# Image rows sent in the steps whose counts they need, and the rest of attention behind the last projection in an order of its own

## The reference

```
h = tok(x);  h = concat([h, txt], axis=1)                      # (32, 144, 192)
Q, K, V = einsum(W_Q|W_K|W_V, layernorm(h))                    # 12 heads of 64
h = h + W_O . (softmax(causal(Q K^T) / 8) V)
logits = layernorm(h) @ Wr;  topk_p, topk_i = top_k(softmax(logits), 2)
counts_before = cumsum(onehot, axis=0) - onehot                # over all rows, in order of the tokens
pos = counts_before at the row's expert;  keep = pos < 864     # capacity
h = h + sum over the 2 experts of  p * keep * (gelu(x @ w1[e] + b1[e]) @ w2[e] + b2[e])
```

## Time and profile before

| | |
|---|---|
| median of 3 runs | 860.81 us (859.82 to 864.62) |
| the profiled execution's own time | 862.2 us |
| its span | 860.5 us |
| attention steps with a projection, one step | 26.0 to 26.4 us |
| start of step 17 on PE | 533 us |
| last merge (pair 17) ends | 604.2 us |
| first load of the experts' block | 638.3 us |

### The profile page before, as it was taken

The page is one execution under the profiler, slowest core; times in us unless marked ns, Lnnn a source line. Parts: engine busy times, 40 slices in busy tenths (PEclk is TensorE's granted clock), DMA queues, the critical chain, the costliest instruction groups (busy, mean ns, idle before and its releaser), DMA issues. The chain is left out here.

```text
span 860.5 us, 25391 instructions
## 1 busy us (share of the span) xinstructions
PE 735.7 (85%) x9539; PEld 611.6 (71%) x9539; DVE 639.1 (74%) x1831; ACT 590.9 (69%) x1383; POOL 512.7 (60%) x612
## 2 busy tenths in 40 slices
PE   3689489999999999999999999975106899999994
PEld 3689257888788888888888888864103577777774
DVE  6892368899999999999999999876304666666651
ACT  1775168888888888888888888862105866766760
POOL 7666325556577687777877777775520154545555
PEclk9899699999999999999999999997557999999998
DMA  8961112111011221222212111220126466664223
GB/s 275 238 164 32 41 57 63 36 37 40 12 45 49 52 58 26 52 52 50 55 34 50 49 40 43 43 59 15 36 83 186 131 132 145 144 145 91 29 28 40
DMA packets 97034, 63.60 MB, mean 74 GB/s; under 512 B 48046, under 2 KB 91547, under 8 KB 96656
## 3 DMA queue, kind: packets, MB, share of 16 engines
q1 hardware_dynamic: 85648, 51.24, 23.0%
q0 software_dynamic: 11264, 10.74, 7.7%
HBM read 39.60 MB, written 24.15 MB: 74 GB/s over the span
## 5 line engine op out<-in xcount | busy, mean ns | idle before, releaser
L1892 POOL DMA_INDIRECT out<-y,tok x56 | 91.6, 1635 | 133.1 <-DVE y L1852 125.2
L1506 POOL TENSOR_TENSOR pl<-p,ph 128x384 f16<-128x384 f32 x144 | 131.6, 916 | 40.5 <-ACT ph L1361 38.0
L1343 ACT ACTIVATE p<-sps,nm 128x144 f32<-128x144 f32 (+1 forms) x432 | 128.7, 390 | 9.9 <-DVE nm L879 9.0
L658 PE MATMUL pj<-xt,wqkvh 128*128 128x256 f16 x648 | 108.4, 277 | 3.9 <-ACT xt L1397 1.5
L1866 DVE TENSOR_TENSOR h<-g,h 128x432 f16<-128x432 f32 x96 | 58.3, 607 | 68.8 <-ACT h L1810 68.7
L1555 POOL DMA_INDIRECT xg_d<-rows,sli x64 | 65.3, 1021 | 43.6 <-DVE sli L1206 34.4
L889 DVE COPY pt<-ptp 128x896 f16<-128x896 f16 (+1 forms) x144 | 86.2, 609 | 4.0 <-PE ptp L719 2.2
L917 DVE SCALAR_TENSOR_TENSOR qk<-pj,qk 128x512 f16<-128x512 f32 x108 | 73.8, 683 | 17.3 <-ACT qk L1326 16.4
L879 DVE TENSOR_REDUCE nm<-sps 128x3 f32<-128x432 f32 (+1 forms) x144 | 82.1, 591 | 4.5 <-PE sps L703 4.2
L1361 ACT ACTIVATE ph<-p 128x384 f16<-128x384 f32 x144 | 74.3, 537 | 15.0 <-PE ptp L719 13.6
L658 PE MATMUL pj<-xt,wqkvl 128*128 128x256 f16 x432 | 83.7, 276 | 0.0
(11 more groups left out here) (251 smaller groups left out, 2394.0 us busy)
## 6 DMA issues: line engine op xcount, KB each, us to landing
stage<-in_L_ffn_w SPq DMA_DIRECT2D x16, 384.0 KB
xg_d<-zrow SPq DMA_DIRECT2D x8, 588.0 KB, 6.1
xg<-xg_d SPq DMA_DIRECT2D x8, 588.0 KB
stage<-in_L_ffn_w SPq DMA_DIRECT2D x8, 576.0 KB, 6.0
out<-h SPq DMA_DIRECT2D x36, 96.0 KB
vi<-vimg_d SPq DMA_DIRECT2D x192, 16.2 KB
hin<-in_txt SPq DMA_DIRECT2D x16, 192.0 KB, 2.9
hres<-in_txt SPq DMA_DIRECT2D x16, 192.0 KB, 3.0
```

The lines of the kernel that those rows point to most:

```text
L658: mm = pe.matmul(bank[:, t * 256:(t + 1) * 256], (wqkvh, wqkvl)[w][:, b, c:c + P], xt[:, q, e, :], start=i == 0, stop=i == 4)
L1343: i = a.activation(p32[:, u % 2, r, lo:SEQ], sps[u % 2][:, r * SEQ + lo:(r + 1) * SEQ], ACT.Exp, bias=nm[:, u % 2, r:r + 1])
L1506: g.tensor_tensor(pl[:, u % 2, :, :], p32[:, u % 2, :, IT:SEQ], ph[:, u % 2, :, :], ALU.subtract).then_inc(S["pll"], 1)
L1892: g.indirect_dma_start(out, bass.IndirectOffsetOnAxis(ap=tok[0:n, 1 - par, u, :], axis=0), y2[0:n, 1 - par, u, :], None, compute_op=ALU.ad ...
```

## The change

Three things are changed. (1) `place_images` is cut into seven parts, `place_img(off, k)`, called for one tile at a time. Tile 0 is done in step 10, tile 1 in step 14 and sent (`send_img`) one step later; tile 2 in step 17; tile 3 at the end. (2) Step 17 (`TAIL`) is the last step of all engines but SP. It holds in one list what was in steps 17 to 22, in a new order. (3) Two waits of PE are finer: scores of units 0 and 1 wait for three items and not six, and pv waits for the one V item that it needs.

```diff
+TAIL = 17
@@ scores
+                if d < 2:
+                    wait(pe, "pjl", 10 * p + 3 * (d + 1))
                 if d == 0:
-                    wait(pe, "pjl", 10 * p + 6)
@@ pv
+                if u % 2 == 0:
+                    wait(pe, "pjl", 10 * p + 7 + u // 2)
                 if u == 0:
-                    wait(pe, "pjl", 10 * p + 10)
@@ step_pe: for s < TAIL as before, and
+            else:
+                scores(1, 0); transpose_a(2, 0, 0); transpose_p(2, 6); pv(2, 5); item(0, 0); transpose_p(2, 7); transpose_a(2, 0, 1); pv(2, 6)
...
+                scores(0, 0); item(0, 5); count(3); pv(1, 4); transpose_p(1, 6); transpose_a(1, 0, 0); item(0, 6); pv(1, 5)
...
+                transpose_p(0, 7); pv(0, 6); transpose_r(1); pv(0, 7); router(1); transpose_a(0, 1, 0); transpose_a(0, 1, 1); merge(0, 0)
+                merge(0, 1); count(1); transpose_r(0); router(0); count(0)
@@ step_dve
+            def place_img(off, k):
+                p = s - off
+                if not live(p) or image_after(p) is None:
+                    return
...
+                if k == 6:
+                    v.tensor_tensor(slia[:, t, :], sla[:, t, :], ova[:, t, :], ALU.add).then_inc(S["sldi"], 1)
...
-            if s == NPAIR:
-                place_images(v, ch, 0, 3)
...
+                logits(0); top(0); top_at(0); shift(0); chosen(0); one_hot(0); total(0); inv_total(0)
+                shares(0); counted(0); both(0); pick(0); inv_both(0); slot(0); fill(0); address(0)
+                place_img(0, 0); send_to(0); place_img(0, 1); next_ids(0); place_img(0, 2); place_img(0, 3); place_img(0, 4); place_img(0, 5)
+                place_img(0, 6)
+        def image_after(p):
+            t, r = divmod(p - NPAIR_A - 3, 4)
+            return t if r == 0 and t >= 0 else None
@@ step_pool
-            if s == NPAIR + 1:
-                wait(g, "sldi", 1)
-                for n in range(6):
-                    send_image(g, *divmod(n, 2))
...
+                send(2, 0, 0); low_a(0, 2); send(2, 0, 1); low_a(0, 3); send_img(4, 0); send(2, 1, 0); send(2, 1, 1); send_img(4, 1)
+                inv_h(0); send(1, 0, 0); send(1, 0, 1); low_r(0); send(1, 1, 0); send(1, 1, 1); send(0, 0, 0); send(0, 0, 1)
+                send(0, 1, 0); send(0, 1, 1); send_img(0, 0); send_img(0, 1)
@@ run
-            for s in range(-1, NPAIR + 5):
+            for s in range(-1, last + 1):
```

More of the change, by code:

```diff
@@ L827, in step_pe @@
                 wait(pe, "init", 1)
[L828 to L865, removed]
@@ L1208, in step_dve @@
             if s == 1:
                 wait(v, "init", 1)
[L1210 to L1272, removed]
@@ L1273, in step_dve @@
-            evac(1, 4)
-            evac(1, 5)
-            counted(3)
-            if s == NPAIR:
-                place_images(v, ch, 0, 3)
[L1279 to L1305, removed]
@@ L1452, in step_act @@
[L1452 to L1472, removed]
@@ L1473, in step_act @@
[L1473 to L1479, removed]
+            if s < TAIL:
+                high_r(3)
+                exps(1, 0)
+                high(0, 0)
+                evac_a(2, 0)
+                exps(1, 1)
+                high(0, 1)
+                cast(1, 0)
+                cast(1, 1)
+                cast_i(1, 0)
+                high(0, 2)
+                cast_i(1, 1)
+                high_a(2, 2)
+                evac_r(3)
+                exps(1, 2)
+                exps(1, 3)
+                high_a(2, 3)
+                high(0, 3)
+                cast(1, 2)
+                high(0, 4)
+                evac_a(2, 1)
+                cast_i(1, 2)
+                cast(1, 3)
+                cast_i(1, 3)
+                high(0, 5)
+                exps(1, 4)
+                exps(1, 5)
+                high(0, 6)
+                high_x(-1)
+                exp_r(3)
+                cast(1, 4)
+                cast_i(1, 4)
+                high(0, 7)
+                cast(1, 5)
+                cast_i(1, 5)
+                high_a(1, 0)
+                put_k(-1, 0)
+                put_k(-1, 1)
+                exps(1, 6)
+                high(0, 8)
+                exps(1, 7)
+                cast(1, 6)
+                high_a(1, 1)
+                cast_i(1, 6)
+                cast_i(1, 7)
+                cast(1, 7)
+                high(0, 9)
+                evac_x(-1)
+            else:
+                high_r(3); evac_a(2, 0); exps(1, 0); exps(1, 1); cast(1, 0); cast_i(1, 0); cast(1, 1); cast_i(1, 1)
+                high_a(2, 2); high(0, 0); exps(1, 2); exps(1, 3); cast_i(1, 2); evac_r(3); cast(1, 2); cast(1, 3)
+                cast_i(1, 3); high_a(2, 3); high(0, 1); exps(1, 4); exps(1, 5); evac_a(2, 1); cast(1, 4); high(0, 2)
+                cast_i(1, 4); cast(1, 5); cast_i(1, 5); high(0, 3); high_a(1, 0); exp_r(3); exps(1, 6); exps(1, 7)
+                high_a(1, 1); cast(1, 6); cast_i(1, 6); high(0, 4); cast(1, 7); cast_i(1, 7); exps(0, 0); exps(0, 1)
+                high(0, 5); evac_a(1, 0); high_r(2); cast(0, 0); cast(0, 1); cast_i(0, 0); cast_i(0, 1); high_a(1, 2)
+                high(0, 6); exps(0, 2); high(0, 7); evac_r(2); exps(0, 3); high_a(1, 3); cast(0, 2); cast_i(0, 2)
+                cast(0, 3); cast_i(0, 3); evac_a(1, 1); high(0, 8); exp_r(2); high(0, 9); high_a(0, 0); exps(0, 4)
+                exps(0, 5); cast(0, 4); cast_i(0, 4); exps(0, 6); cast(0, 5); cast_i(0, 5); cast(0, 6); cast_i(0, 6)
+                exps(0, 7); high_a(0, 1); cast(0, 7); cast_i(0, 7); evac_a(0, 0); high_r(1); high_a(0, 2); evac_r(1)
+                high_a(0, 3); exp_r(1); evac_a(0, 1); high_r(0); evac_r(0); exp_r(0)
@@ L1573, in step_pool, with send_img @@
[L1573 to L1585, removed]
-            if s == NPAIR + 1:
-                wait(g, "sldi", 1)
-                for n in range(6):
-                    send_image(g, *divmod(n, 2))
+            def send_img(off, kk):
+                p = s - off
+                if not live(p) or image_after(p) is None:
+                    return
+                t = image_after(p)
+                wait(g, "sldi", t + 1)
+                send_image(g, t, kk)
@@ L1666, in step_sp, with run @@
                 load_w1(sp, 0, 0)
[L1668 to L1670 removed]
+        def run(f, last=TAIL):
+            for s in range(-1, last + 1):
                 f(s, s % 2)
@@ L1683, in _ @@
                 run(lambda s, par: step_pool(g, s, par))
-                g.wait_ge(S["sldi"], 2)
-                for kk in range(2):
-                    send_image(g, 3, kk)
                 g.wait_ge(S["dsp"], 64 * (NPAIR - NPAIR_A))
```

250 lines of the change are left out of this document (212 added, 38 removed).

## The result

The changed kernel takes 856.36 us (median of 9 runs, 854.44 to 857.78), the kernel before 861.21 (9 runs, 859.82 to 864.62). The ratio is 0.9939 (0.9925 to 0.9954): 4.85 us less, where 14.2 was forecast and the range ended at 855. The profiled execution has a span of 854.2 us against 860.5.

What follows compares the result with a forecast made beforehand. TensorE was taken to bound the middle steps, with no engine full at the end. Gains of 9.5 and 5.7 less 1.0 took 14.2 us from the profiled 862.2, to 848.0, and 846.6 us as median; range 839.5 to 855.

Steps and rivals of the forecast that it cites:

- VectorE's work ahead of the last norm: From the start of step 17 to the last norm: 47.8 us of VectorE work.
- Part one: Tail from step 17 to the last merge: the new order ends the merge 9.5 us earlier (ends 15.4 and 0).
- The 90%: VectorE's busy share from step 17 to the last norm, giving 53.1 us for that stretch.
- The rest of part one: After the last norm: 4.4 us to the first merge, then 4.2 us for the merges.
- Part two: Image transfers at the end: two, not six, ahead of low_r of pair 17; 5.7 us gained (ends 6.4 and 4.5).
- Part three: Tiles 0 and 1 moved into middle steps: 1.0 us lost (0 to 4.4).
- The finer waits: Up to four semaphore waits in each of 16 middle steps: cost 0, bound 3.2 us.
- (b): Tail stays bound by one pair's chain, last norm no earlier: 856.1 us; chance 0.18, with what lies from 852 to 858.
- (c): Single address buffer makes VectorE wait for landed transfers in the last list: slower, up to 869.4 us; chance 0.04.
- signs for being right: Expected residual, low_r and step times, VectorE 85 to 93% busy, clock 1.00 until some 5 us before the merges.
- signs for being wrong: sli waiting over 1 us for a DMA, every middle step 0.2 us longer, or last norm 60 us after step 17's start.

Runs made afterwards that it cites:

- port_moved: The changed kernel with three small VectorE operations between SBUF tiles moved behind the rowmax they held up in the last list; 851.97 us.
- The two probes: The kernel before plus one unused VectorE operation in each of 14 middle steps: two SBUF inputs (867.30 us) or a one-input tensor_reduce (859.77 us).
- best2: best1 plus 36 unused matmuls in TensorE's gaps between the last pv and the two last merges; 848.58 us.
- best1: The kernel before with only the new order from step 17, all image work there, three VectorE operations moved later, token numbers made once at the start; 849.29 us.

## Why the prediction was wrong

The direction was right, the size was three times too large, and the range missed by 1.4 us. The step that failed most is VectorE's work ahead of the last norm, with the price of its waits for GpSimd; the cost in the middle failed with it. By its parts:

- **Part one, tail up to the merge: 9.5 us forecast, 3.4 measured.** The failing term is VectorE's work, 47.8 us. It was 55.2. The 90% that I took was not the error: it was 94%. The 7.4 us between are, but for the precision of my count, waits of small operations for GpSimd, shown as busy: to the last norm long operations exceed the shortest of their form by 10.7 us (11 operations), and 2.2 us of that kind were in the kernel before and so in my count. What I got wrong is their number and size. I took up to 0.6 us each, the remainder of one GpSimd operation, from xn, and 1.8 us in all. Nine of the eleven were of that size (0.3 to 0.75 us over the shortest); one_hot and next_ids were held through several operations, 2.3 and 3.2 us over it. In port_moved, where these two fell to 0.18 and 0.91 us, it is 53.4 us from the start of step 17 (536.4, as far behind the residual in step 16 as in the changed kernel) to the last norm (589.8), where I had forecast 53.1 and the changed kernel has 58.7. I had a rule for these waits: the Trainium skill (SBUF — State Buffer, Who interferes with whom) says that a VectorE instruction with two SBUF inputs contends with a GpSimd instruction that reads SBUF, that one in a two-port mode does too, and that tensor_reduce never does on this chip. The two probes agree with it (up to 2.85 us against 0.15). It speaks of a lock for a whole instruction; these traces show a wait through up to five.
- **The rest of part one held.** From the end of the last norm to the first merge 4.5 us (594.43 to 598.93; forecast 4.4), the merges 4.6 (forecast 4.2). The clock had fallen before them to 0.50 in 597 to 600, as taken. best2 shows 1.6 us for it (4.5 and 2.9 us), but whether transposes count as activity no run here tells apart.
- **Part two, transfers: 5.7 forecast, 6.3 measured**, with low_r where it was expected; no transfer was long.
- **Part three, the middle: 1.0 forecast, 4.3 measured**, the upper end of my range for it (4.4). I had taken VectorE's 1.6 us of idle time in a middle step as cover for 2.0 us of small operations. Step 10 got 2.2 us of busy time more (26.94 against 24.74), and the step is 1.8 us longer. But 1.6 of the 2.2 us are posa and one more address operation (sla, 0.59 and not 0.15 us) standing for GpSimd; that cost I had put at nothing here. Added operations as such were free in the probes' steps. And two transfers that I had called free cost 0.7 us, by what the traces show through xn, which is then held longer by GpSimd's chain. The finer waits cost nothing: middle steps without image work take 26.41 us in both.
- **Rivals.** (b), 856.1, gave the right time for another reason: the last norm did come earlier, by 3.2 us against the start of step 17. So the measured time, within 0.3 us of (b), says nothing for it. (c) did not happen; next_ids stood behind GpSimd's chain, not the address write behind a landing.
- **The signs.** Three of the signs for being right failed: the last residual came 67.9 us behind the start of step 17 and not 60 to 64, steps 10 and 14 were 1.8 and 1.3 us over their neighbours and not within 1, and VectorE was busy for 94% and not 85 to 93. low_r and the clock held. None of the signs for being wrong showed (the last norm came at 58.7 us, just under their 60), so they did not cover this failure.

## What to carry to other kernels

Do not read a duration as work before it is compared with the shortest of its form: here 11.6 us of VectorE's busy time in the tail, and most of what the address operations added to it in step 10, were waits for GpSimd. An operation's price on a nearly full engine depends on where it stands: 0.15 to 0.29 us more in a step with TensorE at 99% and VectorE at 94% were free, and the same probe cost 1.5 to 2.3 us in the three steps where it was held. When two queues are packed more tightly, check which of the short operations between SBUF tiles on VectorE meet chains on GpSimd, and put what the critical path needs ahead of them. Moving three of them won 4.4 us; taking one away won nothing, since the next one waited in its place. A gain is worth what the next queue leaves of it: of the 1.5 us won at the merges nothing came out until GpSimd's transfers had moved, and then 0.9 us at the experts' first load (623.20 against 624.10 in best1).

## What had not been expected of the hardware

A VectorE operation that is held up this way can be held through several GpSimd operations: 2.85 us through five, 3.31 us through the end of a transfer's issue and three. But it can also be let in between two that follow without a gap, as eleven of the fourteen probes were, and one_hot and next_ids in the end. Probes that began at the same point of the same operation (0.24 to 0.27 us before its end) met either; what decides is open. Whether GpSimd's own transfer issue holds it up is open too: one_hot began during one (550.35 to 551.32) and waited, while an operation with two SBUF inputs just ahead of it took 0.16 us.
